# Two value projections of an attention phase moved from the end of a step into its middle, with another order of PSUM banks

## What is computed

```python
def attention(x, mask, adapter, Wq, Wk, Wv, Wo, gate):     # x is layer-normed, adapter is ctx
    q, k, v = (split_heads(x @ W) for W in (Wq, Wk, Wv))
    q, k = rope(q), rope(k)
    w = softmax(q @ k.T / 4 + mask)
    out = w @ v
    a_k, a_v = split_heads(adapter @ Wk), split_heads(adapter @ Wv)
    out = out + tanh(gate) * softmax(q @ a_k.T / 4) @ a_v
    return merge_heads(out) @ Wo
x = x + attention(...)
x = x + experts(layernorm(x))        # top 2 of 8, inner width 352
```

## Time and profile before

| | |
|---|---|
| Median of 3 runs | 2524.99 us (2516.36 to 2528.28) |
| Time of the profiled execution | 2524.06 us |
| Its span, first to last instruction | 2522.1 us |
| Mean granted clock of PE | 0.914 of full |
| PE busy | 2069.4 us (82% of the span) |
| DVE busy | 1444.9 us (57%) |
| ACT busy | 1258.6 us (50%) |
| POOL busy | 821.0 us (33%) |
| Attention phase | up to about 2020 us, 31 steps that prepare a batch, 51.4 to 68.3 us each |
| Expert phase | the last 460 us |

### The profile page before, as it was taken

The page is one execution under the profiler, slowest core; times in us unless marked ns, Lnnn a source line. Parts: engine busy times, 40 slices in busy tenths (PEclk is TensorE's granted clock), DMA queues, the critical chain, the costliest instruction groups (busy, mean ns, idle before and its releaser), DMA issues. The chain is left out here.

```text
span 2522.1 us, 55300 instructions
## 1 busy us (share of the span) xinstructions
PE 2069.4 (82%) x18953; PEld 1234.9 (49%) x18954; DVE 1444.9 (57%) x3715; ACT 1258.6 (50%) x2260; POOL 821.0 (33%) x851
## 2 busy tenths in 40 slices
PE   4888888888788877878788888888888449999997
PEld 2455555544444444544444444544445226666664
DVE  4567666666666666666666666666666433333332
ACT  4565555555555555555455555555555234444443
POOL 2123323233233222232223232222222334444443
PEclk7899989899889888998898989899999769999999
DMA  2001111000000000010000000000001234444444
GB/s 101 21 29 32 30 35 47 29 29 29 29 29 29 29 29 29 29 29 29 29 29 29 29 29 29 29 29 29 29 25 20 52 85 83 84 83 84 83 84 66
DMA packets 69810, 105.95 MB, mean 42 GB/s; under 512 B 25024, under 2 KB 29120, under 8 KB 69120
## 3 DMA queue, kind: packets, MB, share of 16 engines
q0 software_dynamic: 24096, 37.51, 8.6%
q1 hardware_dynamic: 45536, 65.69, 8.4%
HBM read 67.51 MB, written 35.65 MB: 41 GB/s over the span
## 5 line engine op out<-in xcount | busy, mean ns | idle before, releaser
L515 ACT ACTIVATE pr<-st 128x512 f32<-128x512 f32 x512 | 305.0, 596 | 451.0 <-PE st L1083 335.1
L1051 PE MATMUL md<-kk,qz 128*128 128x128 f16 x2048 | 221.1, 248 | 203.1 <-DVE mx L714 79.9
L379 POOL TENSOR_TENSOR t<-t 128x512 f32<-128x512 f32 x64 | 81.4, 1271 | 872.1 <-DVE t L692 872.1
L710 DVE TENSOR_REDUCE mx<-md 128x4 f32<-128x512 f32 x256 | 176.5, 689 | 299.0 <-remote 218.9
L1097 PE MATMUL av<-pr,vv 128*17 128x128 f32 x4096 | 253.6, 293 | 66.4 <-issue 56.1
L1051 PEld LDWEIGHTS md<-kk,qz 128*128 128x128 f16 x2048 | 136.1, 108 | 314.3 <-issue 169.4
L1431 PE MATMUL y<-w1s,hgT 128*128 x1704 | 280.3, 315 | 4.6 <-ACT hgT L1345 4.6
L414 POOL DMA_INDIRECT lists<-row,posi x256 | 248.8, 972 | 86.4 <-issue 86.4
L1074 PE MATMUL st<-qz,kk 128*128 128x256 f16 x1024 | 204.9, 283 | 41.8 <-DVE mT L735 37.1
L507 ACT ACTIVATE qz<-ma 64x256 f16<-64x256 f16 x512 | 191.8, 375 | 79.8 <-remote 65.8
L1431 PEld LDWEIGHTS y<-w1s,hgT 128*128 128x128 f16 x1704 | 164.5, 98 | 96.6 <-issue 5.1
(11 more groups left out here) (200 smaller groups left out, 3875.0 us busy)
## 6 DMA issues: line engine op xcount, KB each, us to landing
wst<-in_w SPq DMA_DIRECT2D x32, 352.0 KB, 3.1
cin<-in_ctx SPq DMA_DIRECT2D x32, 256.0 KB, 4.1
xin<-in_x SPq DMA_DIRECT2D x32, 256.0 KB, 3.8
xres<-in_x SPq DMA_DIRECT2D x32, 256.0 KB, 3.8
out<-x SPq DMA_DIRECT2D x32, 256.0 KB, 2.1
h_pairs<-ohs SPq DMA_DIRECT2D x32, 256.0 KB
lists<-row,posi POOLq DMA_INDIRECT x256
msk<-in_mask SPq DMA_DIRECT2D x32, 64.0 KB, 3.6
```

The lines of the kernel that those rows point to most:

```text
L515: act.activation(pr[:, path, :, :], st[path][:, :, :], ACT.Exp).then_inc(p_ex.sem, 1)
L710: dve.tensor_reduce(mx[:, 1, 4 * g:4 * g + 4], sm[1][:, :, :], AX.X, ALU.max).then_inc(s_ad.sem, 1)
L1051: i = pe.matmul(sm[path][:, j, :], qz[:, h // 2, h % 2, :], keys[:, h // 2, :], start=True, stop=True)
```

## The change

On PE `v(n)` now stands at the end of unit 12, behind `scores(n, 3)`, and `avp(n)` at the end of unit 13, behind `scores(n, 4)`. Both write `ma[1]`. The stacks of the groups 0 to 7 use the banks 0, 1, 0, 1, 0, 0, 0, 1. `avp` waits for ACT's copy of `v` (`v_v`), `stack(n, 7)` for the copy of `avp` (`av_v`). On ACT `own_values` stands in unit 13 ahead of `stack_out(n, 5)`, and `adapter_values` in unit 14 ahead of `stack_out(n, 6)`. `first` gets the same order. No instruction of compute is added or removed.

```diff
+STACK_BANK = (0, 1, 0, 1, 0, 0, 0, 1)
...
         def own_values(n):
             act.wait_ge(v_p.sem, v_p.at(n))
             act.wait_ge(av_pe.sem, av_pe.at(n.shift(-2)))
-            act.activation(vv[:, n.par, 0, :, 0:HD], heads(ma[0]), ACT.Copy, scale=1 / WS).then_inc(v_v.sem, 1)
+            act.activation(vv[:, n.par, 0, :, 0:HD], heads(ma[1]), ACT.Copy, scale=1 / WS).then_inc(v_v.sem, 1)
...
-            bank, pairs = half(ma[g % 2]), slice(2 * g, 2 * g + 2)
+            bank, pairs = half(ma[STACK_BANK[g]]), slice(2 * g, 2 * g + 2)
...
+                if n and u == 13:
+                    own_values(n)
+                if n and u == 14:
+                    adapter_values(n)
                 if u >= 8 and n:
                     stack_out(n, u - 8)
             values_T(b, 3)
-            if n:
-                own_values(n)
-                adapter_values(n)
...
         def x_turn(n):
             pe.wait_ge(x_hi.sem, x_hi.at(n))
             pe.wait_ge(x_lo.sem, x_lo.at(n))
-            pe.wait_ge(v_v.sem, v_v.at(n.shift(-1)))
+            pe.wait_ge(stk_o.sem, stk_o.at(n.shift(-1), GROUPS - 1))
...
         def k(n):
-            pe.wait_ge(av_v.sem, av_v.at(n.shift(-1)))
+            pe.wait_ge(x_T.sem, x_T.at(n))
+            pe.wait_ge(stk_o.sem, stk_o.at(n.shift(-1)))
...
         def v(n):
-            pe.wait_ge(stk_o.sem, stk_o.at(n, GROUPS - 1))
-            project(ma[0], xT, wv).then_inc(v_p.sem, 1)
+            pe.wait_ge(stk_o.sem, stk_o.at(n, 4))
+            project(ma[1], xT, wv).then_inc(v_p.sem, 1)
 
         def avp(n):
-            pe.wait_ge(stk_o.sem, stk_o.at(n))
+            pe.wait_ge(v_v.sem, v_v.at(n))
             project(ma[1], cT, wv).then_inc(av_p.sem, 1)
...
-            if g >= 2:
+            if g in (2, 3, 4):
                 pe.wait_ge(stk_o.sem, stk_o.at(n, g - 1))
...
+            if g in (5, 6):
+                pe.wait_ge(stk_o.sem, stk_o.at(n, g))
+            if g == 7:
+                pe.wait_ge(av_v.sem, av_v.at(n))
+            bank = ma[STACK_BANK[g]]
...
                 if u >= 9 and n:
                     scores(n, u - 9)
+                if u == 12 and n:
+                    v(n)
+                if u == 13 and n:
+                    avp(n)
             values(b, 2 * GROUPS - 1)
             if n:
                 scores(n, GROUPS - 1)
-                v(n)
-                avp(n)
```

More of the change, by code:

```diff
@@ L606, in first @@
             for g in range(GROUPS):
+                if g == 5:
+                    own_values(n)
+                if g == 6:
+                    adapter_values(n)
                 stack_out(n, g)
-            own_values(n)
-            adapter_values(n)
             x_turned(n.shift(1))
@@ L1035, in stack @@
                 pe.wait_ge(f_cnt.sem, f_cnt.at(n.shift(-3)))
-            if g >= 2:
+            if g in (2, 3, 4):
                 pe.wait_ge(stk_o.sem, stk_o.at(n, g - 1))
-            turn_pairs(qs, ma[g % 2], 0, 2 * g, 2)
-            turn_pairs(ks, ma[g % 2], 2, 2 * g, 2)
-            turn_pairs(aks, ma[g % 2], 4, 2 * g, 2).then_inc(stk_t.sem, 1)
+            if g in (5, 6):
[3 more added lines that the diff above has]
+            bank = ma[STACK_BANK[g]]
+            turn_pairs(qs, bank, 0, 2 * g, 2)
+            turn_pairs(ks, bank, 2, 2 * g, 2)
+            turn_pairs(aks, bank, 4, 2 * g, 2).then_inc(stk_t.sem, 1)
         def scores(n, g):
@@ L1191, in first @@
                     stack(n, g + 1)
+                if g == 3:
+                    wait_weight(3)
+                    v(n)
+                if g == 4:
+                    avp(n)
                 scores(n, g)
```

## The result

| | before | with the change |
|---|---|---|
| Median | 2526.64 us (4 runs, 2516.36 to 2531.44) | 2584.35 us (4 runs, 2581.09 to 2591.01) |
| Ratio | | 1.0237 (95% interval 1.0199 to 1.0276) |
| Profiled execution, its span | 2524.06, 2522.1 us | 2583.1, 2581.1 us |
| Mean granted clock of PE | 0.914 | 0.898 |
| PE, DVE, ACT, POOL busy | 2069.4, 1444.9, 1258.6, 821.0 us | 2063.5, 1446.8, 1248.5, 821.4 us |

A forecast was written before the change was run, and what follows sets the result against it. PE bounds a step's first half; later the PE-DVE exchange, updates late beside POOL's list DMAs, and the end projections do. 29 x (-3.2 + 1.7 + 3.5) = +58, plus 10, on 2524.06 gave 2590 us, range 2488 to 2642.

The forecast's parts named there:

- End of the step: Between `scores(n, 7)` and the next step: with the projections gone DVE's chain lasts, a mean of 3.2 us less per step.
- Middle: Units 12 to 15: `avp` waits behind the late `exps(b, 13)`, maxima 5 start later, 1.7 us more per step.
- the nearest row: Stack update sent at 1745.6 beside the list DMAs, 3.7 us late; taken as the delay of the `scores_T(b, 13)` update.
- Start of the next step: `scores_T`, `q` and `k` behind the new idle time at the end: a fall of the clock costing 1.75 us.
- The jump: End of an iteration: the 1.68 us of PE between `max_turn` and the next `scores_T` were kept unchanged.
- Steps without lists: The first pass and steps 0 and 1: 3.4 us longer each, three times, +10 us.
- That PE's updates get through: Rival beside the lists: updates pass at once, the middle costs 0, one clock fall is left; 2492 us, chance 0.20.
- That they are held until the lists are through: Rival beside the lists: `exps(b, 13)` only at 1753.70, everything 2.1 us later; 2653 us, chance 0.13.
- that rival: Rival on PE's clock: one fall per step instead of two, about 2541 us, or none, about 2486; chance 0.20.

The follow-up runs named there:

- e7: The changed kernel with `mT` copied ahead of `normal(b, 3)` on DVE; 2557.8 us, ratio 1.0125.
- e2: The changed kernel with POOL's eight list DMAs held until `mT`; 2570.2 us, ratio 1.017.
- e5: The changed kernel with `own_values` ahead of `exps(b, 13)` on ACT; 2547.8 us, ratio 1.0078.
- e6: e1 with the list DMAs in two fours, four where they were and four behind `mT`; 2344.1 us, ratio 0.9276.
- e9: The kernel before with the list DMAs in two fours, the second four behind `mT`; 2407.5 us, ratio 0.9498.
- e4: The changed kernel with one more, unread projection at the end of each step, ahead of `values_back`; 2520.3 us, ratio 0.9983.
- e10: The changed kernel with the list DMAs in two fours; 2441.2 us, ratio 0.9645.
- e8: The changed kernel with one more, unread projection per step, behind `max_turn`; 2568.1 us, ratio 1.0148.
- e1: The kernel before with only `v` moved to the middle, `avp` staying at the end of the step; 2499.4 us, ratio 0.9894.

## Why the prediction held

The forecast was 2590 and the slower side, the measurement is 2584.35. The directions and the waits were as told, but that the sum came so close is luck: what I put too high in the middle of a step (1.0 us) and too low at its start (0.4 us of clock, 0.7 us of jump) cancelled.

- **End of the step**, -3.2 us: measured -3.3. The chain neg_max, normal, `mT` ends it, as e7 confirms.
- **Middle**, +1.7 us and a fall of the clock of 1.75: the first stretches (+0.4 and +3.3) and the shorter one behind them (-1.3) make +2.5 in all, against 3.45. The mechanism was as told: `exps(b, 13)` late, the copy behind it, `avp` behind both (e2, e5). The delay was 2.75 us and not the 3.7 of the nearest row, the wait 3.15 (2.91 on average) and not 4.2. The update is sent 5.9 us behind the start of the lists, as I had laid it, but `v` sends nothing for 2.6 us ahead of it, so fewer updates stood before it than before the stack's of the earlier trace rows. That this makes it 2.75 and not 3.7 fits e6 and e9, and was not tried by itself. The clock fell over `avp` in 10 of the 29 steps only: `avp` takes 3.22 us on average, 0.62 more, not 1.75. What I had left at nothing was the pace of DVE behind it. Maxima 5 to 7 take 5.37 us instead of 6.67, at a granted clock of 0.80 on average instead of 0.63; that the one makes the other is likely and not shown.
- **Start of the next step**, a fall of the clock of 1.75: it came in every one, and cost 1.2 us ahead of `q` and 1.0 over it, 2.2 us (e4 takes both away where no jump comes between).
- **The jump.** "At the end of an iteration PE also shows 1.68 us between `max_turn` and the next `scores_T`, which I keep". This step failed. In the kernel before `max_turn` waits for nothing, and 2.14 us pass from its start to the next `scores_T`. Once it waits for `mp`, it is 3.98 us, and about the same (3.9 to 4.0) in e2, e5, e7 and e10, where it waits too; the gap grows from 1.86 to 3.56 us. That is 1.7 us in 12 steps, 20 us, and 0.7 a step. My reading is that without the wait PE's stream runs ahead of the array into the jump while `avp` is still computed. e8 fits it, but no run moves the wait alone, and e1, where `max_turn` waits in one of the 12 steps only, has a gap of 2.95 us that it leaves open.
- **Steps without lists**: +10 forecast, +4.4 measured (0.8, 4.7 and -1.1).
- **Rivals.** That PE's updates get through is refuted by the 2.75 us; and e10 shows that the change would not pay then either, which I had not seen: I let `avp` lie wholly beside DVE's idle time, but with punctual updates that idle time is gone. That they are held until the lists are through applies to the updates of the stack and of `scores(n, 4)` (5.3 and 4.6 us), not to the one that `avp` hangs on. The clock fell twice in a third of the steps and once in the others, so that rival was partly true, and the jump made up for it.

The Trainium skill (Advanced Engine Details and Errata, DMA Bandwidth Details) puts an increment at about one cycle of overhead. Where POOL issues no lists, nothing here speaks against it: 0.03 us pass from matmul to exponential in e2. Beside the lists the update took 2.75 us, so the figure is no guide to when an update arrives. I had also written that by it `avp` would not wait at all; it waits 0.43 us for the copy even with punctual updates (e2).

## What to carry to other kernels

Before moving work into an engine's idle time, ask what makes the time idle: here it was a series of eight indirect DMAs on another engine, and splitting that series in two was worth 120 to 155 us, where moving the projections cost 58 or gave 28. If work has to go there, move the part that waits for nobody and sends nothing until it is done (`v`), and leave the part that waits for a copy of it (`avp`) where it covers an end; put the copy ahead of whatever waits for a slower signal. Look at what stands in front of a loop's jump: behind a wait it took longer here, and useful work queued behind the last wait could fill that time (e8 filled it with work that nobody reads).

## What the runs showed of the hardware

- Updates from PE to ACT and DVE are delayed beside a series of indirect DMAs that POOL issues, and the delay grows with the number issued before them: 0.3 to 1.0 us beside the first ones (`scores_T(b, 13)` before, in 26 of the 29 steps), 2.7 to 6.2 us beside the later ones of eight, up to 2.1 us with four (e9), and 0.03 us behind a first one followed by a pause. I had expected the delay, not that it depends so much on the length: two series of four cost 4 to 6 us a step less than one of eight.
- Across the jump of the loop PE's matmuls start 3.98 us apart behind an instruction that waits (with the change, 3.56 us of it idle), and 2.14 us apart behind one that doesn't (before, 1.86 us idle). Queued matmuls of 2.75 us leave 0.9 to 1.5 us idle (e8).
- An engine with more work made the kernel faster: 31 unread projections gave 64 us (e4), mostly since PE came to the next step at 2.4 GHz instead of 1.2: the start of a step up to maxima 3 is 2.4 us shorter. A part of it is the shorter gap behind the jump, 0.84 us in 12 steps.
